# Causal rounds: first half of the value products ahead of the scores in every step

## The reference

```python
q = q * cos + _neg_half(q) * sin          # k likewise
scores = jnp.einsum('btghk,bThk->bghtT', qg, k)
mask = jnp.tril(jnp.ones((t, t), bool))
scores = jnp.where(mask, scores, -jnp.inf) / np.float32(np.sqrt(K))
p = jax.nn.softmax(scores, axis=-1)
out = jnp.einsum('bghtT,bThv->btghv', p, v).reshape(b, t, HQ * V)
return out @ wo
```

## Time and profile before

| | |
|---|---|
| median of 3 runs | 1313.04 us (1310.7 to 1314.91) |
| profiled execution | 1311.32 us, span 1309.5 us |
| PE busy | 1118.2 us (85%) |
| DVE busy | 1048.1 us (80%) |
| POOL busy | 1000.8 us (76%) |
| ACT busy | 870.7 us (66%) |
| PE busy from 400 to 600 us | 196.45 us, granted clock 1.00 |

### The profile page before, as it was taken

How to read it: one execution, slowest core, us unless ns; L and a number is a source line. 1 busy time by engine, 2 the same in 40 slices (tenths; PEclk the granted TensorE clock), 3 DMA queues, 4 the chain that set the end, 5 groups by cost and what they waited for, 6 DMA issues and landing times.

```text
span 1309.5 us, 36076 instructions
## 1 busy us (share of the span) xinstructions
PE 1118.2 (85%) x14984; PEld 839.0 (64%) x14984; DVE 1048.1 (80%) x2168; ACT 870.7 (66%) x1508; POOL 1000.8 (76%) x795
## 2 busy tenths in 40 slices
PE   4979886899999999999999999999999997500981
PEld 2777783466776767767677776776767776500881
DVE  6587765889898898989989889888898875692665
ACT  3656572598888888888889888888888894100330
POOL 3555875599898988989899898898888996236454
PEclk8889997899999999999999999999999998555995
DMA  6250002221221311213112131121211200031793
GB/s 221 47 146 2 2 18 85 70 77 39 69 59 45 77 38 53 63 57 78 38 53 62 42 93 38 54 62 50 69 38 27 62 3 2 0 114 60 221 299 143
DMA packets 49246, 90.84 MB, mean 69 GB/s; under 512 B 8896, under 2 KB 19136, under 8 KB 48832
## 3 DMA queue, kind: packets, MB, share of 16 engines
q1 hardware_dynamic: 46128, 81.21, 21.7%
q0 software_dynamic: 2960, 7.38, 2.2%
HBM read 43.96 MB, written 13.01 MB: 44 GB/s over the span
## 4 chain that ended last, share of the span: by engine, by line
PE 61%; DVE 20%; POOL 7%; issue 4%; SPq 3%; ACT 3%; DMA 2%; POOLq 0%; DVEq 0%; ACTq 0%
PE psT L1131 6%; PE psS L1206 5%; PE psS L1205 5%; PE psS L1227 5%; PE psS L1228 4%; PE psT L1119 4%; PE psS L1229 4%; PE psT L1154 3%; PE psO L1206 3%; PE psO L1205 3%; PE psO L1131 3%; DVE pmax L1609 3%; POOL rows_in L741 2%; PE psO L1119 2%; DVE psT L1586 2%
## 5 line engine op out<-in xcount | busy, mean ns | idle before, releaser
L713 POOL TENSOR_TENSOR probs<-arena,probs 128x512 f16<-128x512 f32 x576 | 656.5, 1162 | 93.0 <-ACT probs L911 90.2
L911 ACT ACTIVATE probs<-arena 128x512 f16<-128x512 f32 x576 | 361.2, 627 | 14.6
L1227 PE MATMUL psS<-vb,probs 128*128 128x65 f16 x2304 | 302.3, 192 | 3.4 <-POOL probs L713 1.2
L1228 PE MATMUL psS<-vb,probs 128*128 128x64 f16 x2304 | 303.6, 194 | 0.0
L1229 PE MATMUL psS<-vb,probs 128*128 128x65 f16 x2304 | 301.7, 192 | 0.0
L923 ACT ACTIVATE arena<-psS 128x512 f32<-128x512 f32 x384 | 225.9, 588 | 94.3 <-PE psS L1206 54.7
L1227 PEld LDWEIGHTS psS<-vb,probs 128*128 128x128 f16 x2304 | 220.1, 97 | 67.3 <-issue 10.5
L1228 PEld LDWEIGHTS psS<-vb,probs 128*128 128x128 f16 x2304 | 215.4, 97 | 50.9
L1609 DVE TENSOR_REDUCE pmax<-psT 128x1 f32<-128x512 f32 (+1 forms) x341 | 218.8, 645 | 26.3 <-PE psT L1134 13.6
L1229 PEld LDWEIGHTS psS<-vb,probs 128*128 128x128 f16 x2304 | 216.7, 98 | 0.0
L1131 PE MATMUL psT<-arena 128*128 128x512 f16 (+3 forms) x507 | 158.1, 330 | 2.7 <-DVE pmax L1611 2.1
(11 more groups left out here) (278 smaller groups left out, 2889.3 us busy)
## 6 DMA issues: line engine op xcount, KB each, us to landing
arena<-arena SPq DMA_DIRECT2D x240, 128.0 KB, 2.4
arena<-w_exp_dram SPq DMA_DIRECT2D x40, 384.0 KB, 4.2
arena<-xnT_d SPq DMA_DIRECT2D x16, 512.0 KB, 3.7
wkv<-w_d SPq DMA_DIRECT2D x16, 352.0 KB, 4.2
rows_in<-arena POOLq DMA_DIRECT2D x1, 2580.0 KB, 20.3
arena<-rows_in SPq DMA_DIRECT2D x40, 64.5 KB, 3.4
arena<-x_dram SPq DMA_DIRECT2D x4, 512.0 KB, 5.2
hres<-x_dram SPq DMA_DIRECT2D x4, 512.0 KB, 4.9
```

What stands on the lines that cost most here:

```text
L713: pool.tensor_tensor(pl[:, r, :], pf[:, r, :], ph[:, r, :], ALU.subtract).then_inc(lo_P, 1)
L911: act.activation(ph[:, s % RING, :], pf[:, s % RING, :], ACT.Copy).then_inc(b_hi, 1)
L1227: pe.matmul(dst, high, vb[:, p, j, 0:OW], start=first, stop=False, skip_group_check=True)
L1228: pe.matmul(dst[:, 0:HD], high, vb[:, p, j, HD + 2:VW], start=False, stop=False, skip_group_check=True)
```

## The change

In every step PE does the first half of the value products first, then waits for the exponential as before and does the scores, then the first side entry, the second half, and the other entries. There is one order for all steps, whatever their number of entries; the wait is moved into `scoresB`.

```diff
             def scoresB(it, p, s):
                 g, c = divmod(s, SPH)
+                if s >= SCORES or it > 0:
+                    pe.wait_ge(b_exp, it * SPR + s - SCORES + 1)
                 if c == 0:
                     pe.wait_ge(row_in, 16 * (it * G + g) + 16)
...
                 for s in range(SPR):
-                    if s >= SCORES or not first:
-                        pe.wait_ge(b_exp, it * SPR + s - SCORES + 1)
-                    scoresB(it, p, s)
                     n = len(steps[s])
                     todo = [lambda k=k: side(work, k, base, p, it, prior) for k in range(i, i + n)]
                     i += n
...
-                    if n == 1:
-                        order = parts[0:1] + parts[1:2] + todo
-                    else:
-                        order = todo[0:1] + parts[0:1] + todo[1:2] + parts[1:2] + todo[2:]
+                    order = parts[0:1] + [lambda s=s: scoresB(it, p, s)] + todo[0:1] + parts[1:2] + todo[1:]
                     for f in order:
                         f()
```

## The result

| | before | changed |
|---|---|---|
| median of the first comparison | 1311.92 us (4 runs) | 1341.12 us (1338.86 to 1344.63, 4 runs) |
| profiled execution, span | 1311.32, 1309.5 us | 1338.86, 1337.0 us |
| ratio to before | | 1.0227, 95% interval 1.0198 to 1.0256 |

The changed kernel is 2.3% slower. A second comparison of the same two kernels (e11) gave 1.0256, interval 1.0234 to 1.0278. Predicted were 1346 us and a range of 1333 to 1356 us.

What follows compares the result with a forecast made beforehand. PE was taken to bound the causal rounds, so only its waits could move the time: +34.5 - 2.2 + 0.4 = +32.7 us, giving 1346 us from the median, 2.5% slower; 8-in-10 range 1333 to 1356 us.

Steps and rivals of the forecast that it cites:

- (b): Steps 5, 14, 23, 32: a new head's value products wait for DVE's normalised output of the head before; +34.5 us.
- (a): Value products' wait for POOL's low probabilities: 3.1 us of room at step 23, late only in first round; 0.4 us allowed.
- (c): PE's waits for DVE to read side-entry banks: those at step 6 shrink, -2.2 us; entries after step 25 taken as 0.
- rival 1: DVE gets maxima 0.36 us earlier at one-entry steps 3 and 12, delivers earlier: about 1327 to 1337 us; 12%.
- Rival 2: Waits spread: later entries behind the new waits find DVE bunched, 5 to 19 us on top, 1351 to 1365 us; 10%.
- rivals 3 and 4: 3: DVE runs ahead from steps 0 to 6, 1302 us, 3%; 4: PE's later waits shrink equally, no measurable change, 2%.
- rival 5: Clock swings: an 8 us stretch of each round falls to 0.71, 37 us on top, 1383 us; 2%.
- rival 3: Faster: DVE runs ahead from steps 0 to 6, PE's waits for L1588 and L1609 go, 11 us, 1302 us; 3%.

Runs made afterwards that it cites:

- e11: Changed kernel once more, unedited, for more runs against the kernel before: 1344.39 us, ratio 1.0256.
- e2: Kernel before, but at steps 5, 14, 23 and 32 alone the first half goes ahead of the scores: 1334.22 us, ratio 1.0197.
- e1: Changed kernel, but at steps 5, 14, 23 and 32 the first half stays behind scores and first entry: 1313.68 us, 1.0024 of before.
- e3: Changed kernel; on DVE bank 1's reciprocal and L1644 go ahead of the side entries of steps 3, 12, 21, 30: 1310.75 us, 1.0001 of before.
- e8: Changed kernel; on DVE only L1644's product of steps 21 and 30 goes ahead of the second entry: 1327.52 us, 1.0121 of before.
- e4: Kernel before; only in the 13 one-entry steps the entry directly follows the scores, both halves behind it: 1309.18 us, ratio 1.0006.
- e9: Changed kernel; at a head's start PE's wait for DVE's normalised output is written ahead of that for low probabilities: 1339.57 us, 1.0214 of before.
- e5: Kernel before with DVE's reciprocal and L1648 for bank 1 ahead of the side entries of steps 3, 12, 21, 30: 1310.59 us, ratio 0.9988.
- e7: Kernel before with e5's edit and PE's projections-done signal to SP moved to the end of step 21: 1304.21 us, ratio 0.9941.
- e10: Changed kernel with e3's edit and PE's projections-done signal to SP moved to the end of step 21: 1306.90 us, 0.9967 of before.

## Why the prediction was right

**The step that carried it held.** "Every V now belongs one place further on", and the wait for DVE's L1648 that "had hardly any room" ends last at the four steps at which a head begins: waits of 0.65, 0.24, 1.11 and 0.30 us for 0.64, 0.22, 1.09 and 0.29 predicted. The sum of (b), +34.5 us, is 37.0 - 2.3 = 34.7 us. e2 shows that these steps make most of the loss by themselves and e1 that the other steps without them make little; e3 that it is DVE's place for L1644, and e8 that it acts step by step. Nine of the 63 places lie over 0.06 us off the figure of their step: in round 0 step 23 waited 0.40 us and step 32 1.14 where 1.54 was written, step 14 of round 6 waited 1.23 us, two places at step 32 only 0.05, and the four of round 15 were off by 0.2 to 0.3 us either way. Together they cancel to some 0.1 us, so that the sum fits to 0.2 us is in part luck; the size of the usual wait at each step is not.

**(a)**: low probabilities had room. By the signals in the profile after, the shortest within the rounds 1 to 15 was 0.43 us. In round 0 one value product, at step 31, was released by them and lost less than 0.02 us of the 0.4 us allowed for; with DVE out of the way (e3) the same place waits 0.41 us. Behind the last step of round 15, where the last value products stand alone, two more wait for them in both kernels: 0.36 and 0.77 us before, 0.55 and 0.77 us in the changed kernel.

**(c)**: at step 6, -2.2 us predicted, 2.9 - 0.7 = 2.2 us measured. At step 25 I had taken nothing, and nothing came in the changed kernel; e8 shows how small the room there is.

**One-entry steps** don't matter (e4), so rival 1 falls, whose mechanism they were. Rival 2 put 1351 us or more and falls with the medians of 1341 and 1344 us, rivals 3 and 4 fall with the result, rival 5 with the granted clock of 1.00 in the rounds. (The 11 us of rival 3 take each of the 26 waits at the longest, 0.3 us; by the row they are 6.6 us, so 9.5 with L1609's, and nothing hangs on it.) Gaps of 0.2 to 1.1 us in every round did not make the clock swing. The rule of the Trainium skill that the prediction weighed ("TensorE: Matmul & The Clock Gate", "A second HAM failure mode: psum-queue depth-cycling") does not bite here.

**What was off.** First, the total: +32.7 us predicted for the whole, +31.4 measured in the causal part, and +27.5 in the profiled execution, since the routing gave 3.1 us back and the part behind it 0.7. Those parts were no term of the sum at all. By the medians it is +29.2 us in the first comparison and +33.0 in the second; the profiled execution of the changed kernel was the quickest of its runs both times, and where the slower ones spend their time no profile shows. Inside the causal part the waits named make 34.7 - 2.2 = 32.5 us; the 1.1 us that are missing lie in other waits of PE that shrank and were not taken one by one. Second, two signs I had named for being right or wrong: the added waits were to be put down "to issue or to L1648", and I was to be wrong if the value products waited for L713 "in more than a handful of steps". The page names L713 57 times. Taken by the letter this sign spoke against a mechanism that e3 and e9 show; the sign was badly chosen, since this wait is for two semaphores, and the view of the weight loads names the one that the load itself carries (e9), whichever ended last; the old one of step 23 stood under "issue".

## What to carry to other kernels

Before a half-step of work is moved ahead in an engine's order, list every semaphore that it waits for and read the room of each at the new place, in every phase of the pattern: here one wait had 3 us and the other, in 4 steps of 36, none. A stall of the engine that bounds the kernel can be cured on the other engine's side, by the place of the instruction that it waits for; here either order did then (e3 and e5, e7 and e10). Of two waits of one instruction, write the one that ends last so that the instruction itself carries it; here that was the one written first.

## What the runs showed beside it

- **A releaser can be the wrong one.** With the order of two waits swapped and nothing else, 42.8 us "for POOL" became 36.2 us "for DVE". The start of the waiting instruction against the ends of both candidates decides.
- **The second wait costs.** A wait as an instruction of its own on PE let the value product start 0.135 us after the signal, one carried by the weight load 0.045 to 0.047 us, in 61 places each.
- **The time of the routing takes steps.** Over the thirteen profiled kernels it took 52.2, 55.4 or 58.5 us, with the same instructions. PE's granted clock goes to and fro between 1.2 and 2.4 GHz there, and how much of PE's work falls on which level differs: in the profiles with 52.2 us the second stretch at 2.4 GHz is the longest, in those with 55.4 us it is half as long, in those with 58.5 us it is missing. Differences of 3 us between kernels of this kind can come from there; the causal part by itself tells them apart.
